# Transposes of quantised rows by DMA: row tiles 0 to 2 ahead of the gate product, row tile 3 ahead of the last down product

## What is computed

```python
def rms_norm(x, w):
    var = jnp.mean(x * x, axis=-1, keepdims=True)
    return x * jax.lax.rsqrt(var + EPS_NORM) * w

def activation_quant(x):
    scale = 127.0 / jnp.clip(jnp.max(jnp.abs(x), axis=-1, keepdims=True), EPS_Q, None)
    return jnp.clip(jnp.round(x * scale), -128, 127) / scale

def bitlinear(x, w, norm_w):          # weights are quantised to -1, 0, 1 times a scale
    ...
    return jnp.einsum('bsh,oh->bso', xq, wq)
y = bitlinear(x, w_gate, norm_gate)   # 1024 -> 2 x 2816
gate, up = jnp.split(y, 2, axis=-1)
h = gate * jax.nn.sigmoid(gate) * up
return bitlinear(h, w_down, norm_down)  # 2816 -> 1024
```

## Time and profile before

| | us |
|---|---|
| median of 3 runs | 631.88 |
| lowest, highest | 631.66, 632.05 |
| profiled execution | 631.64 |
| its span, first to last instruction | 629.8 |

### The profile page before, as it was taken

One profiled execution on the slowest core, in us unless ns is written; L12 is line 12 of the kernel. 1 busy time (PEld: TensorE's weight loads), 2 busy tenths in 40 slices (PEclk: granted clock), 3 DMA queues, 4 the chain that ended last, 5 costly groups with the idle time before them and its releaser, 6 DMA issues.

```text
span 629.8 us, 10610 instructions
## 1 busy us (share of the span) xinstructions
PE 611.2 (97%) x3624; PEld 477.2 (76%) x3625; DVE 508.6 (81%) x885; ACT 425.9 (68%) x560; POOL 193.5 (31%) x174
## 2 busy tenths in 40 slices
PE   7999999998999999999998999999999999999996
PEld 6778888887887444444556788898988989889775
DVE  5888888888787787989898569688796887969677
ACT  3998888889755989887575357558384573846630
POOL 2345446426000333426930220040330404214052
PEclk9999999999999999999999999999999999999999
DMA  8977776765246997936999658796876968769457
GB/s 336 401 303 301 308 304 241 309 266 200 101 143 259 417 356 265 407 134 250 400 360 425 236 223 294 250 363 247 301 290 236 367 222 329 278 248 350 135 171 272
DMA packets 31070, 177.91 MB, mean 282 GB/s; under 512 B 4064, under 2 KB 4064, under 8 KB 14784
## 3 DMA queue, kind: packets, MB, share of 16 engines
q1 hardware_dynamic: 25536, 158.64, 65.9%
q0 software_dynamic: 5504, 18.88, 8.3%
HBM read 154.30 MB, written 23.20 MB: 282 GB/s over the span
## 4 chain that ended last, share of the span: by engine, by line
PE 65%; ACT 14%; DVE 13%; issue 4%; DMA 3%; POOL 1%; DVEq 0%; POOLq 0%; ACTq 0%
PE BK L2174 11%; PE BK L307 10%; PE BK L1896 4%; PE BK L319 4%; PE BK L2177 4%; PE BK L313 4%; ACT RA L1390 4%; ACT PR L1417 4%; PE BK L314 4%; PE BK L2144 3%; PE BK L1939 3%; PE BK L2132 2%; PE BK L1841 2%; DVE WL L1038 2%; PE BK L2130 2%
## 5 line engine op out<-in xcount | busy, mean ns | idle before, releaser
L2174 PE MATMUL BK<-EX,WH 128*128 128x320 f32 x384 | 99.4, 342 | 0.0
L705 POOL TENSOR_TENSOR WL<-RC,WH 128x2048 fp32r<-128x2048 f32 x7 | 45.5, 6503 | 167.8 <-ACT WH L1598 167.8
L1038 DVE TENSOR_TENSOR WL<-RA,WH 128x2048 fp32r<-128x2048 f32 x40 | 89.4, 2286 | 9.2 <-ACT WH L1598 8.8
L2177 PE MATMUL BK<-EX,WL 128*128 128x160 f32 x336 | 79.2, 236 | 0.0
L1598 ACT ACTIVATE WH<-RA 128x2048 fp32r<-128x2048 f32 x40 | 73.6, 1905 | 0.1
L2174 PEld LDWEIGHTS BK<-EX,WH 128*128 128x128 f32 x384 | 69.2, 189 | 0.0
L2177 PEld LDWEIGHTS BK<-EX,WL 128*128 128x128 f32 x336 | 64.1, 191 | 0.0
L655 POOL TENSOR_TENSOR HB<-HB,ND (+2 forms) x26 | 28.7, 1120 | 100.4 <-DVE BH L922 99.8
L1489 ACT ACTIVATE RA<-RA,RT 128x2048 int16<-128x2048 f32 x22 | 43.8, 1999 | 3.6 <-DMA RA<-wbit 1.8
L1705 ACT ACTIVATE HX<-SR 128x320 fp32r<-128x320 f32 x16 | 7.6, 472 | 57.0 <-DVE SR L1088 57.0
L1896 PE MATMUL BK<-TG,XQ 128*128 128x512 bf16 x192 | 42.4, 379 | 0.1
(11 more groups left out here) (333 smaller groups left out, 1671.6 us busy)
## 6 DMA issues: line engine op xcount, KB each, us to landing
RA<-wbit SPq DMA_DIRECT2D x54, 1024.0 KB, 6.6
RA<-wmoe SPq DMA_DIRECT2D x40, 1024.0 KB, 6.5
RC<-wmoe SPq DMA_DIRECT2D x20, 1024.0 KB, 8.0
rows<-ZERO POOLq DMA_DIRECT2D x40, 256.0 KB, 8.3
XG<-rows SPq DMA_DIRECT2D x10, 512.0 KB, 3.6
rows<-YS SPq DMA_DIRECT2D x9, 512.0 KB, 4.4
RA<-wqk SPq DMA_DIRECT2D x7, 640.0 KB, 8.5
RA<-wo SPq DMA_DIRECT2D x4, 1024.0 KB, 7.3
```

What stands on the lines that cost most here:

```text
L705: e.tensor_tensor(WL[2][:, at], RC[5][:, :], WH[2][:, at].bitcast(f32), ALU.subtract).then_inc(free_c[5], 1)
L1038: e.tensor_tensor(WL[m][:, q * RAW:q * RAW + RAW], RC[j][:, :], WH[m][:, q * RAW:q * RAW + RAW].bitcast(f32), ALU.subtract)\
L2174: mm = e.matmul(bank[GBK[f]][:, 0:2 * R], WH[m][:, at], EX[:, k, :, :].rearrange("p a b -> p (a b)"), start=k == 0, stop=k == KD - 1)
L2177: e.matmul(bank[GBK[f]][:, 0:R], WL[m][:, at], EX[:, k, 0, :], start=False, stop=False)
```

## The change

Tiles 0 to 2 of ZQ are no longer transposed on TensorE. ScalarE's queue issues a transposing DMA for each from ZQ[t % 2] to XQ (`rows_turned`), at the places where `rows_out` stood. Each raises a semaphore of an earlier load, which stands at 16, to 32; TensorE waits for it before the gate block of the tile, and VectorE's `gate_rows(2)` and `gate_rows(3)` wait for the transfers of tiles 0 and 1 before they write ZQ again. Tile 3 stays on TensorE and ScalarE. In the down product tile 3 of HQ goes by one transposing DMA to HQT[0], issued by ScalarE behind the root of router tile 0, once HQ is written (`hq` = 10) and the products of tiles 0 and 1 are done (`d_pe` = 4). TensorE's `hidden_t(3)` and ScalarE's copies of it are gone.

```diff
@@
-HTB = ((2, 3, 2), (2, 3, 2), (2, 3, 4), (5, 4, 2))
-HTW = ((None, None, 1), (3, 2, 4), (6, 5, None), (None, 9, 7))
+HTB = ((2, 3, 2), (2, 3, 2), (2, 3, 4))
+HTW = ((None, None, 1), (3, 2, 4), (6, 5, None))
+XQ_IN, HQ_IN = ("x_in0", "x_in2", "ctx_in"), "ctx_in2"
@@ VectorE, gate_rows
                 if t >= 2:
-                    e.wait_ge(s("zt_pe"), t - 1)
+                    e.wait_ge(s(XQ_IN[t - 2]), 32)
@@ ScalarE
+            def rows_turned(t):
+                e.wait_ge(s("zq"), t + 1)
+                e.dma_start(XQ[:, :, t * P:t * P + P], ZQ[t % 2][:, :], transpose=True).then_inc(s(XQ_IN[t]), 16)
+
             def rows_out(t):
-                e.wait_ge(s("zt_pe"), t + 1)
+                e.wait_ge(s("zt_pe"), 1)
@@
-            rows_out(0)
+            rows_turned(0)
...
-            rows_out(1)
+            rows_turned(1)
...
-            rows_out(2)
+            rows_turned(2)
@@
-            hidden_t(3)
+            e.wait_ge(s("hq"), 10)
+            e.wait_ge(s("d_pe"), 4)
+            e.dma_start(HQT[0][:, :, :], HQ[:, :], transpose=True).then_inc(s(HQ_IN), 16)
@@ TensorE
                 wout(t, 1, range(KD), True, True).then_inc(s("y_tile"), 1)
-                rows_t(t - 1)
@@
-                if c == 0:
-                    e.wait_ge(s("xq"), t + 1)
+                if c == 0 and t < NT - 1:
+                    e.wait_ge(s(XQ_IN[t]), 32)
+                elif c == 0:
+                    e.wait_ge(s("xq"), 1)
@@
-                    e.wait_ge(s("hq"), 3 * t + q + 1 if t < 3 else 10)
+                    e.wait_ge(s("hq"), 3 * t + q + 1)
@@
-            hidden_t(3)
             e.wait_ge(s("x3"), 1)
             down_part(2, 1, 0, KB)
-            e.wait_ge(s("hqt"), 12)
+            e.wait_ge(s(HQ_IN), 32)
```

## The result

| | us |
|---|---|
| before, median of 4 runs | 631.77 (631.13 to 632.05) |
| after, median of 4 runs | 658.34 (653.03, 655.31, 661.37, 661.75) |
| after to before | 1.041, 95% interval 1.037 to 1.045 |
| profiled execution after, its span | 655.31, 653.5 |

The change costs 26.6 us on the median, far outside the range, in the direction of the rival that I had given 0.05. The four times fall into two pairs, 653 and 655 us and 661 and 662 us, and the median lies between them; those of before are within 1 us of each other. The profiled execution belongs to the early pair, 23.7 us above before, and is explained first. The spread is a second effect, taken up in the last experiments.

The account below looks back on a forecast made before the run. It took the end of the projections to bound around 195 to 212 us and the DMA engines, filled by ZERO's writes, at 343 us; -0.9 + 2.4 = +1.5 on 631.88 gave 633.4 us, range 630.9 to 637.5.

Parts of the forecast that it names:

- The landing of the big transfer: Tile 3 of HQ, down product: lands 7.6 us after its issue, at 315.0, 0.7 us late for VectorE.
- The 4.6 us until the first packet: Down product: a new queue under ZERO's load starts moving 4.6 us after its issue, read from loads issued at 322.72.
- block after block: Rival, big transfer: small pieces each wait among ZERO's packets; landing 330.7, VectorE 16.4 us late, +15.5, 647.4 us; chance 0.05.
- X-Bar Transpose as fast as ordinary DMAs: Skill page's estimate for the big transfer: 350 to 400 GB/s, holding the engines 1.8 to 2.1 us for 704 KB.
- place A: End of the projections, 195 to 212 us: eight transposes fewer for each of tiles 0 and 1 save 0.86 us, taken as -0.9.
- ZERO displaced: Forecast case, 300 to 350 us: the big transfer displaces its own bytes, ZERO's writes end 2.4 us later; chance 0.40.
- Place B: 300 to 350 us, tile 3 of HQ and ZERO's writes: DMA engines bound the copy at 343.00; the change costs +2.4 us.
- The signs: Right: residual 199.6, matmuls 210.9, landing 7 to 8 us, TensorE idle 3. Wrong: late tile 1 root, ZERO's end before 343.
- TensorE's 1.23 us gain nothing: Down product, tile 3: TensorE loses 22 transposes, 1.23 us, but VectorE is the bound there, so gain nothing.
- ScalarE held: Issue of the big transfer at 307.4: 5.7 us of holding is free; held until 315.0, VectorE would be 1.9 us late.
- cost nothing: Three small transfers of ZQ, 173 to 205 us: price nothing, with 5.2 us for the third and 19 us for the first.

Follow-up runs that it names:

- the last experiments: Gate-row transfers only, HQ on TensorE: tiles 0 and 2, ratio 1.000; tile 1, 0.999; all three with later loads held back, 0.9985, or issued by SyncE, 0.9983.
- the pause kernel: Changed kernel with gate rows on TensorE; GpSimd issues 8 of ZERO's 40 writes, waits for HQ's transfer to land, then issues the other 32: 647.15 us.
- the kernels that hold ZERO back: Changed kernel with all 40 ZERO writes after the big transfer's landing: 665.51 us; with gate rows on TensorE and 32 writes after it: 647.15 us.
- the late case: Traced execution of the changed kernel with all 40 ZERO writes issued only after the big transfer's landing; tile 1's small transfer took 18.7 us; 665.51 us in all.

## Why the prediction was wrong

**The landing of the big transfer** is the step that failed. I took it at 7.6 us, from the rate in bytes of a load under ZERO (0.285 MB/us). It was 30.3 us. The rows had half of the answer: from 328 to 332 us the loads had 155 packets and ZERO 157. I read their MB, 1.14 and 0.51, as shares. What is shared is the number of turns; the loads got more bytes because their packets carry 7.4 KB against ZERO's 3.3 KB. A transposing transfer, with 256 bytes in a packet, gets a thirtieth of what the loads get; its packet size stood in no row of before. The Trainium skill has the rule in "DMA: Bandwidth & Descriptors", section Queues, rings and completion order: each DMA engine goes round the queues that have work, a whole packet at a time. The trace agrees as far as its counts go, 394 to 396; they are sums over the 16 engines. The 4.6 us until the first packet nearly held: the first 18 came between 310 and 311 us, behind an issue at 306.0.

**The rival "block after block"** named the right direction and, in its words about turns among ZERO's packets, the right mechanism. Its price was a loan, the longest landing of a ZERO write (23.3 us, +15.5), and its evidence, the Trainium skill's 1309 ns for a block in "VectorE: DVE Perf Modes", section The three transpose paths, is not what acts here: alone a block takes 0.24 us. That the 28.8 us worked out from that page lie near the measured landing is chance. I gave the rival 0.05 because 16 engines work side by side; they do, and each waits for its own turns.

**X-Bar Transpose as fast as ordinary DMAs** (the Trainium skill, "Advanced Engine Details and Errata", section X-Bar Transpose (TRN2)): this does not hold here. With the engines to itself the transfer of the pause kernel moves 0.22 MB from 309 to 310 us, 220 GB/s, where ZERO alone moves 0.36 MB/us and the page gives 350 to 400 GB/s. Beside another queue it is 0.09 to 0.10 MB in 4 us.

**The sum as it came out,** with the landing in it: the product of tile 3 would have been wanted by the second half of the residual at 324.5 - 1.2 = 323.3, and with the full clock would have come at 336.3 + 9.7 = 346.0, 22.7 us late. The lower clock adds 2.2 us, a term I did not have; place A takes off 1.2. Together +23.7, the growth of the span in the profiled execution. The median of +26.6 has the late executions in it.

**ZERO displaced,** my forecast (+2.4 us): it did not come about. The transfer did not displace its own bytes: from 312 to 316 us ZERO moved 1.14 MB, where it had moved 1.45 in 4 us, so it lost 0.31 MB while the transfer got 0.09. And everything behind the product moved by more than that, so that ZERO was no bound at all. In the kernels that hold ZERO back it was the bound, by 13.9 us for the pause, but there the edit's own wait delays it, not the bytes of the transfer. Place B lost in both ways that were tried: the transfer waits or ZERO does.

**The signs.** Of those named for a right forecast, the two of place A came (199.21 and 210.59), the three of place B did not: landing 30.3 us instead of 7 to 8, TensorE idle 25.6 us instead of some 3, VectorE not waiting for ZERO. Two of those named for a wrong one came: the root of tile 1 late (the reciprocal at 329.41, before at 314.52), and ZERO through before 343.

**TensorE's 1.23 us gain nothing:** right, as the pause kernel shows. **ScalarE held:** I asked whether 5.7 us were enough; it was 22.0 us, and harmless only because the product was later still.

**Place A.** Right in its chain, with two errors. The size: 1.23 us instead of 0.86. The matmul behind the transposes of tile 0 was itself followed late, at 178.11 instead of 178.03, so a block costs about 0.5 us and not 0.43; some 0.1 us was there before the place began (projection matmuls at 175.66 and 175.78). In the times of the kernels with all three small transfers and without the big one the gain is 0.6 to 0.9 us where they are not late. And the small transfers "cost nothing": I showed room in slices of 15.7 us and time before the result is needed. The slice from 188 to 204 us stands at 6, but in windows of 4 us the loads of the kernel before hold 91% of the engines from 188 to 192 and 102% from 192 to 196. What the transfers do to those loads I left out. Landings of 10.5 and 10.2 us beside loads and 3.1 us without were within the room; the late case, 18.7 us, was not.

## What to carry to other kernels

Before a transfer of short packets is put beside a full queue, count packets, not bytes: as long as the other queue stays full, its time is about its packets per engine times the duration of a pair of packets, one of each queue. The DMA view gives both, and equal packet counts of two queues in one window are the sign of it. Here a transposing DMA did well where the engines were idle, and in the queue of the loads that run beside it; and when an engine that is not the bound is relieved by it, there is nothing to win.

## What the runs showed of the hardware that I had not expected

- The issue of a transposing DMA of 704 KB holds its engine's queue for 3.4 us when the transfer runs alone and for 16 to 23 us beside ZERO as it was (ScalarE 15.8 and 22.0, SyncE 22.7); with ZERO in other pieces it was 10.0 to 23.8 us. One of 256 KB holds it for 1.2 to 1.5 us, with loads beside it or without.
- A transposing DMA from SBUF to SBUF moves 0.22 MB/us with the engines to itself, ZERO's plain writes 0.36 MB/us.
- Shorter rows do not make shorter packets: ZERO's 3200 packets stayed, each only slower (0.145 us with rows of 4 KB, about 0.2 us with rows of 512 bytes).
- Transposing packets from one queue and load packets from another can slow each other beyond their turns: 0.36 MB of loads in 4 us at a busy share of 83%, in the one late execution that was traced. By the times, 6 of 11 executions of one kernel were late, and none of 11 when a single queue issued both.
